# Moving the first counts' bounds and two batch-end steps of a top-k search to GpSimd, and reading the next quad's first maxima one mask earlier

## What is computed

```python
k = _crucial_k(C)                      # 38 of 1601 (C = 64 rows of x are kept)
cm = jnp.moveaxis(channel_map, 1, 2)   # (16, 2048, 1601)
_, topk_idx = jax.lax.top_k(cm, k)
mask = jnp.zeros((B, L, C), x.dtype).at[b_idx, l_idx, topk_idx].set(1.0)
crucial_features = crucial_channels * x
subcrucial_features = subcrucial_channels * x
c_max = jnp.max(crucial_features, axis=1, keepdims=True)
...
return crucial_features * A_S1 + subcrucial_features * A_S2
```

## Time and profile before

| | us |
|---|---|
| median of 3 runs | 2283.42 (2282.82 to 2288.04) |
| the profiled execution | 2279.7 |
| its span | 2277.9 |
| DVE busy over the span | 1402.7 (62%) |
| ACT busy | 1013.3 (44%) |
| POOL busy | 1021.4 (45%) |
| PE busy | 2004.4 (88%) |

### The profile page before, as it was taken

One profiled execution on the slowest core, in us unless ns is written; L12 is line 12 of the kernel. 1 busy time (PEld: TensorE's weight loads), 2 busy tenths in 40 slices (PEclk: granted clock), 3 DMA queues, 4 the chain that ended last, 5 costly groups with the idle time before them and its releaser, 6 DMA issues. The chain is left out here.

```text
span 2277.9 us, 39061 instructions
## 1 busy us (share of the span) xinstructions
PE 2004.4 (88%) x15226; PEld 1633.7 (72%) x15226; DVE 1402.7 (62%) x2179; ACT 1013.3 (44%) x2014; POOL 1021.4 (45%) x930
## 2 busy tenths in 40 slices
PE   4778788777764947999999999999999999999999
PEld 3666566555554836787877888878778878888887
DVE  6999999999999989844444531144445425731111
ACT  7778788877840355423222422223223322422221
POOL 1223332222226522755564456556555445644554
PEclk9999999999987869999999999999999999999999
DMA  9999999889930114632225443322244345434443
GB/s 382 375 355 378 337 323 322 318 293 319 333 145 15 75 43 132 185 107 75 80 97 181 139 145 109 94 83 77 83 161 144 126 136 213 131 129 125 140 139 117
DMA packets 158392, 407.69 MB, mean 179 GB/s; under 512 B 15616, under 2 KB 44544, under 8 KB 156544
## 3 DMA queue, kind: packets, MB, share of 16 engines
q1 hardware_dynamic: 157920, 403.55, 51.7%
q0 software_dynamic: 288, 1.64, 0.2%
HBM read 379.96 MB, written 25.17 MB: 178 GB/s over the span
## 5 line engine op out<-in xcount | busy, mean ns | idle before, releaser
L1238 POOL TENSOR_TENSOR t<-t,t 128x512 fp32r<-128x512 f32 (+1 forms) x488 | 652.5, 1348 | 658.7 <-ACT t L1231 585.5
L1789 PE MATMUL ps<-t,t 128*128 128x512 f32 x1856 | 737.6, 397 | 12.4 <-POOL t L1238 7.1
L1791 PE MATMUL ps<-t,t 128*128 128x512 f32 x1856 | 723.8, 390 | 0.0
L1790 PE MATMUL ps<-t,t 128*128 128x512 f32 x1856 | 723.1, 390 | 0.0
L693 PE MATMUL ps<-t,t 128*128 128x128 bf16 (+1 forms) x6656 | 450.1, 221 | 181.3 <-DVE t L440 163.3
L1231 ACT ACTIVATE t<-t 128x512 fp32r<-128x512 f32 (+1 forms) x488 | 296.2, 608 | 696.1 <-PE ps L1791 381.6
L693 PEld LDWEIGHTS ps<-t,t 128*128 128x128 bf16 x6656 | 386.4, 100 | 279.8 <-DVE t L440 248.0
L440 DVE TENSOR_SCALAR t<-t,t 128x1601 bf16<-128x1601 f32 x512 | 516.2, 1050 | 4.6 <-DVE t L601 0.9
L642 ACT ACTIVATE t<-t,t 128x1601 bf16<-128x1601 f32 x256 | 416.9, 1628 | 62.7 <-DVE t L585 59.0
L1789 PEld LDWEIGHTS ps<-t,t 128*128 128x128 f32 x1856 | 348.3, 188 | 92.7 <-POOL t L1238 11.6
L1791 PEld LDWEIGHTS ps<-t,t 128*128 128x128 f32 x1856 | 348.3, 188 | 74.1
(11 more groups left out here) (210 smaller groups left out, 1692.9 us busy)
## 6 DMA issues: line engine op xcount, KB each, us to landing
t<-ctxT SPq DMA_DIRECT2D x256, 800.5 KB, 6.4
t<-wqkv SPq DMA_DIRECT2D x192, 256.0 KB, 3.1
t<-wo SPq DMA_DIRECT2D x128, 256.0 KB, 4.5
t<-wb SPq DMA_DIRECT2D x128, 256.0 KB, 3.5
t<-xT SPq DMA_DIRECT2D x48, 256.0 KB, 6.7
t<-x1d SPq DMA_DIRECT2D x32, 256.0 KB, 4.8
x2d<-t SPq DMA_DIRECT2D x32, 256.0 KB, 2.0
t<-x2d SPq DMA_DIRECT2D x8, 1024.0 KB, 7.4
```

The source lines that it names most:

```text
L1238: e.tensor_tensor(wlo[r][:, 0:nk, :], raw[r][:, 0:nk, :], wh[r][:, 0:nk, :].bitcast(F32), ALU.subtract).then_inc(w_lo, 1)
L1789: e.matmul(bank[:, :], wh[r][:, q, :], xl, start=(kt == 0), stop=False)
L1790: e.matmul(bank[:, :], wlo[r][:, q, :], xh, start=False, stop=False)
L1791: m = e.matmul(bank[:, :], wh[r][:, q, :], xh, start=False, stop=(c == NCH[p] - 1 and q == nk - 1))
```

## The change

The bounds leave DVE: a function `bounds_gpsimd` issues the same operation on POOL, once before the copy of a quad's tile 0 and once before the copy of its tile 2. `maxima(0)` of quad i+1 moves from the head of step i+1 to step i, ahead of its last mask (after the seventh, `done == 7`). The batch's end steps are numbered anew: the fill of `thr` is step 0 and the conversion of the sums is step 1, and both are issued by POOL for batches 0 to 14 (`fin_gpsimd`, in POOL's program right after the first bounds of step 4b+6). DVE's part begins with step 2 after the third mask. PE's, ACT's and SP's programs are the same as before.

```diff
@@ -441,6 +441,7 @@
 
     def fin_vector(e, b, steps):
         y, rows_ = b % 2, slice(16 * b, 16 * b + 16)
         third = slice(16 * b + 4, 16 * b + 20)
         vv = v8[:, y, :, :]
@@ -448,13 +449,13 @@
             if s:
                 e.wait_ge(fin, NF * b + s)
             if s == 0:
+                i = e.memset(thr[y][:, :], FMAX)
+            if s == 1:
                 i = e.tensor_copy(sumsu[:, third], sums[:, third])
-            if s == 1:
+            if s == 2:
                 i = e.tensor_scalar(sumsu[:, third], sumsu[:, third], int(HIGH) - 1, None, ALU.bitwise_and)
-            if s == 2:
+            if s == 3:
                 i = e.tensor_scalar(sumsu[:, third], sumsu[:, third], float(K), None, ALU.is_lt)
-            if s == 3:
-                i = e.memset(thr[y][:, :], FMAX)
             if s == 4:
                 i = e.copy_predicated(thr[y][:, :], insA[:, rows_], vv[:, :, 3])
             if s == 5:
@@ -569,22 +570,15 @@
             def end_batch(s):
                 if bf is not None and s is not None:
                     fin_vector(e, bf, s)
-            b, t0 = tile_of(4 * i)
-            y = b % 2
-
-            def maxima(half):
+            def maxima(i, half):
+                b, t0 = tile_of(4 * i)
                 if half == 0 and b >= 2 and t0 == 0:
                     e.wait_ge(fin, NF * (b - 1))
                 for u in (2 * half, 2 * half + 1):
                     landed(e, 4 * i + u)
-                    e.max(v8[:, y, t0 + u, :], ring[(4 * i + u) % NR][:, 0:C]).then_inc(maxed, 1)
-
-            def bounds(half):
-                n, two = 4 * i + 2 * half, slice(t0 + 2 * half, t0 + 2 * half + 2)
-                e.wait_ge(maxed, n + 2)
-                e.tensor_scalar(nT[:, n:n + 2], v8[:, y, two, 3], TINY, -1.0, ALU.max, ALU.mult).then_inc(bound4, 1)
-            if i < NQ:
-                maxima(0)
+                    e.max(v8[:, b % 2, t0 + u, :], ring[(4 * i + u) % NR][:, 0:C]).then_inc(maxed, 1)
+            if i == 0:
+                maxima(0, 0)
             if 1 <= i <= NQ:
                 g = i - 1
                 gb, gt = tile_of(4 * g)
@@ -592,8 +586,6 @@
                 e.wait_ge(signed, 4 * g + 4)
                 e.tensor_scalar(insA[:, 4 * g:4 * g + 4], cntA[:, 4 * g:4 * g + 4], 2.0 * K - CM - 1.0, None,
                                 ALU.is_lt).then_inc(a_dec, 1)
-            if i < NQ:
-                bounds(0)
             if 1 <= i <= NQ:
                 e.wait_ge(a_dec, g + 1)
                 e.wait_ge(tied, g + 1)
@@ -612,23 +604,25 @@
                 e.wait_ge(counts_out, slot_of(i - 1, 3) + 1)
                 e.tensor_scalar(insB[:, 4 * c:4 * c + 4], sums[:, 4 * c:4 * c + 4], HIGH * K, None, ALU.is_lt).then_inc(b_dec, 1)
                 e.wait_ge(b_dec, c + 1)
-                end_batch([0] if first_steps else [7])
+                end_batch([] if first_steps else [7])
                 w = insB[:, 4 * c:4 * c + 4]
                 e.copy_predicated(vc[:, :, 0], w, vc[:, :, 2]).then_inc(b_set, 1)
-                end_batch([1] if first_steps else [8])
+                end_batch([] if first_steps else [8])
                 e.wait_ge(b_set, c + 1)
             done = 2
             if i == 0 or i == 1:
-                maxima(1)
-                bounds(1)
+                maxima(i, 1)
+            if i == 0:
+                maxima(1, 0)
             for k, (kind, u) in enumerate(masks_of(i)):
                 if kind == "b" and u < 2:
                     continue
                 mask_vector(e, i, kind, u, vg[:, u, 1:2] if kind == "b" else vc[:, u, 0:1])
                 done += 1
                 if 2 <= i < NQ and done == 3:
-                    maxima(1)
-                    bounds(1)
+                    maxima(i, 1)
+                if 1 <= i < NQ - 1 and done == (4 if i == 1 else 7):
+                    maxima(i + 1, 0)
                 if first_steps and i <= NQ + 1 and done <= 7:
                     end_batch([done - 1])
                 if k == 4:
@@ -663,6 +657,21 @@
             if 1 <= i <= NQ + 1:
                 counts_scalar(e, i, 2)
 
+    def bounds_gpsimd(e, i, half):
+        n = 4 * i + 2 * half
+        b, t = tile_of(n)
+        e.wait_ge(maxed, n + 2)
+        e.tensor_scalar(nT[:, n:n + 2], v8[:, b % 2, t:t + 2, 3], TINY, -1.0, ALU.max, ALU.mult).then_inc(bound4, 1)
+
+    def fin_gpsimd(e, b):
+
+        e.wait_ge(fin, NF * b)
+        e.memset(thr[b % 2][:, :], FMAX).then_inc(fin, 1)
+        e.wait_ge(b_dec, 4 * b + 5)
+        e.wait_ge(fin, NF * b + 1)
+        third = slice(16 * b + 4, 16 * b + 20)
+        e.tensor_copy(sumsu[:, third], sums[:, third]).then_inc(fin, 1)
+
     def quad_gpsimd(e, i):
 
         b, t0 = tile_of(4 * i)
@@ -675,6 +684,10 @@
     def search_gpsimd(e):
         for n in range(B * NT):
             b, t = tile_of(n)
+            if n % 2 == 0:
+                bounds_gpsimd(e, n // 4, n % 4 // 2)
+            if n % 4 == 0 and n // 4 >= 6 and (n // 4 - 6) % 4 == 0:
+                fin_gpsimd(e, (n // 4 - 6) // 4)
             if b >= 2 and t == 0:
                 e.wait_ge(fin, NF * (b - 2) + 8)
             landed(e, n)
```

## The result

| | before | after |
|---|---|---|
| median, us | 2284.97 (13 runs) | 2277.59 (13 runs, 2272.14 to 2282.84) |
| ratio of the times | | 0.9973, 95% interval 0.9966 to 0.9981 |
| the profiled execution, us | 2279.7 | 2278.36 |
| its span, us | 2277.9 | 2276.6 |
| last decision of count A in the search | 660.56 | 658.51 |

The change makes the kernel faster by 0.27%, 6.2 us by the ratio (4.3 to 7.8 by its interval). That is just under the 0.3% that I had set as the limit, inside the range (2274 to 2291) and inside the forecast's own range (2276 to 2289), and clearly more than the 1.1 us of my sum. One of the 13 executions of before took 3285.11 us, far from all others, and is not in the ratio of the fast ones. The two profiled executions differ by 1.3 us only; what stands between 1.3 and 6.2 took experiments of its own.

What follows compares the result with a forecast made beforehand. DVE's own program was taken to set the time up to about 680 us. Terms -12.4 + 1.0 + 5.8 + 2.5 + 2.0 = -1.1 us, against 2279.7 profiled and median 2283.4, gave about 2282; range 2274 to 2291.

Steps and rivals of the forecast that it cites:

- The second half's saving: DVE, maxima of tiles 2 and 3 to the next mask: 0.26 instead of 0.46 us, 62 x 0.20 = 12.4 us saved.
- The first half's saving: DVE at a step's head: the bounds leaving there lay under a wait, and moved maxima cost the same; gain 0.
- POOL held to 0.09 after the mask's end: Second half's bounds on POOL wait out a mask; sign 2 is 0.85 us later, 16 odd steps lose 0.36: +5.8 us.
- POOL in the gaps: POOL operations where DVE turns to a mask lengthen masks, 0.04 us a step: 62 x 0.04 = +2.5 us.
- the second rival: POOL passes first at three gaps a step, 0.08 us each: 14.9 instead of 2.5, 2295 us; chance 0.15.
- The batch's end: DVE's renumbered batch steps now stand between masks: +0.07 us in 15 batches, +1.0 us.
- The DMAs: Maxima of tiles 0 and 1, read 1.23 us earlier, and a faster DVE wait for DMAs: +2.0 us.
- the ACT term: Decision B waits for ACT's late counts, 0.36 us in 16 odd steps from 25 to 55: +5.8 us.
- the first (full gain, 2274): POOL's bounds slip ahead of the mask, or ACT has more reserve: -6.9 to -11 us, 2274; chance 0.20.
- The third (the DMAs early on): DMAs bound the early search, nothing saved before 240 us: DMA term 4.4 + 2 instead of 2.0, 2287; chance 0.12.

Runs made afterwards that it cites:

- u_bnd1: The changed kernel with the bounds of tiles 2 and 3 back on DVE, right after their maxima: 2283.23 us, ratio 0.9996 to the kernel before.
- sq_early: The changed kernel with the layer norm's square moved in ACT's program from behind count 1 to ahead of sign 2: 2274.61 us, ratio 0.9958 to before.
- sq_gap: As sq_early, and POOL also waits for a step's first mask before copying tiles 0 and 1: 2274.01 us, ratio 0.9962 to before.
- u_fin: The changed kernel with the batch's end wholly on DVE as before, no fill or conversion on POOL: 2276.79 us, ratio 0.997 to before.
- before3: Third profiled execution of the unchanged kernel before: 2284.06 us, clock 0.973, the search's last decision A at 663.99.
- early: The changed kernel with the maxima of tiles 2 and 3 one mask earlier, ahead of the third mask: 2290.3 us, ratio 1.0031 to before.

## Why the prediction was right, and where it was off

Right was the mechanism of the larger terms, to the place. The size of the net change was not: the sum named 1.1 us of the 6.2, and the time lies inside the range because the range was wide for so small a net. Each step with what the traces of after (two) and before (four) show:

- The second half's saving, 62 x 0.20 = 12.4 us: measured about 13 (12.9 and 12.8 in the two pairs of traces, 12.9 in the sum below) as the sum over all steps from the maxima to the next mask. u_bnd1 shows that the gain hangs on it.
- The first half's saving, 0: right; L587 to L593 is 0.20 to 0.21, and from decision A to the first mask the 63 steps add up to 26.1 us, 26.3 to 26.5 before.
- POOL held to 0.09 after the mask's end, sign 2 at 1.43 after the maxima: measured 1.40, and the decision B late in the 16 even steps from 26 to 56: 0.27 instead of 0.36. 4.3 us instead of 5.8. sq_early shows its cause; why it was 0.27 and not 0.36 no run takes apart. The prediction's last line calls the odd steps the long ones; the wait falls in the even ones (2.61 against 2.40), as its list of signs has it.
- POOL in the gaps, 2.5 us: the lengthened masks add up to 2.5 us in both traces of after (45 and 44 masks), but before had 10 to 16 such masks and 0.4 to 0.9 us already, so the change costs about 1.8. sq_gap shows the cause. A sign that the prediction gave to the second rival came up: masks over 1.10 us in most steps (41 of 62). It was one mask a step and not three, so it did not decide. The prediction took the lock rule that the Trainium skill states in "SBUF — State Buffer", section "SBUF: two separate sides", to hold the mask for the operation's whole 0.23 us, 14 us in all. But by that rule the mask waits only until POOL's operation ends, and the masks above fit it if a mask takes the port 0.20 after its recorded start, which is worked out from their lengths and not seen by itself.
- The batch's end, +1.0: about 0. u_fin is level with after.
- The DMAs, +2.0: the maxima's waits after 27 us rose from 2.2, 1.8, 0.8 and 1.6 in the four of before to 3.7 and 3.7, +2.1.
- Not in the sum: the start. The second decision A came at 27.65 and 27.41 us, not at 26.45 to 26.87: +0.9, with 0.7 us of waiting for ACT (the one row of L587 in the waits above).

By these the sum is -12.9 + 4.3 + 1.8 + 0.0 + 2.1 + 0.9 = -3.8 us, where it was -1.1: the ACT term was 1.5 too big, the batch's end 1.0, the gaps 0.7, and the saving 0.5 too small, while the start's 0.9 was missing. This agrees with the mean of the profiled executions: 2282.3 for four of before, 2278.3 for two of after. With the two quick ones of before alone it does not agree: they are only 1.6 us slower than after.

The rest of the miss is not in the terms. The prediction read all its rows in one profiled execution, 2279.7, and set its sum on it and on the median as if the two were of one kind. This one was a quick one of before, with few stretches at half clock. The search's end in after, 658.51, is only 2 us earlier than in it; against before3 it is 5.5.

What is left, about 2 to 4 us between the -3.8 or -4.0 of the traces and the -6.2 and -7.5 of the runs, stays open. The four profiled executions of before lie 2 us under the mean of the 23 others, those of after 1 us over the mean of theirs; with so few, this may be chance. The 13 and 6 executions of after had a mean clock of 0.9736 and 0.9740 and the 23 of before 0.972; 0.001 of the mean clock goes with 0.8 us in these 23 (0.5 in the 17 on the second chip), so that 1 to 1.6 us go with the clock. Why after should meet fewer of the stretches, or bear them better, no run here tells apart.

Of the rivals, the first (full gain, 2274) is wrong in its reason: the second half's bounds were held in every step. Its time is what sq_early reaches, by the cure of the loss that it denied. Its -11 needed the gaps' 2.5 us gone as well; with the 5.8 and the 2.0 alone it is -8.9. The second (slower, POOL in the gaps) needed more than 0.06 a step and got 0.04. The third (the DMAs early on) was too pessimistic for this kernel, but early shows how near it was: one mask.

## What to carry to other kernels

Before a small operation goes from a full VectorE to GpSimd, look where it will fall. It is held to the end of the VectorE mask that started ahead of its signal, so whoever waits for it gets it a mask later; the gain is then the wait that left VectorE, less what the late signal costs behind. All of this was seen here for small operations beside the 128x1601 masks. Pay that cost with work which the waiting engine can do in the meantime: moving the square of 0.62 us into ScalarE's wait was worth 2 to 3 us more in the times of the runs and about 4 in the traces, beside 6 to 7.5 of the change.

And look at the granted clock of the profiled execution beside those of the timed ones: a forecast of a few microseconds laid on one execution can be off by more than itself.

## What the runs showed of the hardware that I had not expected

A GpSimd operation queued behind the mask stream runs at one per mask: bounds, two copies and a comparison took 0.94, 1.89 for two, and 0.99 us, each ended about 0.1 us after a mask, and the masks went on undelayed (four in 3.93). In a gap of 0.69 us the same bounds took 0.22.

A GpSimd operation of up to 0.24 us that begins in VectorE's short gap or up to 0.04 us behind a mask's recorded start mostly passes (376 of 439 that started within 0.04 us after a mask), and then costs the mask only what it lasts beyond 0.20 us after that start: 0.06 us here, not 0.24. None of those that started 0.06 us or more after it (within 0.30) passed.

In a kernel whose search is bound by VectorE, a fall of TensorE's granted clock to 1.2 GHz goes with lost time too, 0.5 us and more at a time, through counts that come late and mask buffers that are freed late. The executions of the kernel before differ by 8 us, and in the 23 on one chip about half of the scatter goes with the mean clock.
